# A step of self attention with its matrix products in another order

## The reference

```
scores = einsum('bhqd,bhkd->bhqk', q * 16**-0.5, k)      # 16 heads of 16 features
scores = where(causal, scores, finfo.min)
p   = softmax(scores, axis=-1)
ctx = einsum('bhqk,bhkd->bhqd', p, v)
```

## Time and profile before

| | us |
|---|---|
| median of three runs | 3683.33 |
| lowest and highest of them | 3674.78, 3687.11 |
| the profiled execution | 3663.53 |
| its span, from first to last instruction | 3661.7 |
| mean granted TensorE clock in the span | 0.972 of full |

### The profile page before, as it was taken

How to read it: one execution, slowest core, us unless ns; L and a number is a source line. 1 busy time by engine, 2 the same in 40 slices (tenths; PEclk the granted TensorE clock), 3 DMA queues, 4 the chain that set the end, 5 groups by cost and what they waited for, 6 DMA issues and landing times. The chain is left out here.

```text
span 3661.7 us, 74050 instructions
## 1 busy us (share of the span) xinstructions
PE 3383.0 (92%) x25048; PEld 2302.3 (63%) x25048; DVE 2019.3 (55%) x3324; ACT 1840.3 (50%) x3374; POOL 1590.0 (43%) x1421
## 2 busy tenths in 40 slices
PE   7777889898999799989999999999999998999997
PEld 5544644444444388866666666666666666878886
DVE  4454477777777455435555555555555553113454
ACT  2244357676776633435555555555555553333333
POOL 3211222121122111115777777777777776004554
PEclk9899989999999999999999999999999999999998
DMA  4765300000000123230010100000001002210200
GB/s 121 166 102 93 132 5 18 17 18 17 17 18 27 40 112 117 92 125 7 13 34 13 32 13 31 13 32 13 31 13 58 15 13 97 95 70 14 97 7 12
DMA packets 74751, 179.36 MB, mean 49 GB/s; under 512 B 14720, under 2 KB 44928, under 8 KB 68480
## 3 DMA queue, kind: packets, MB, share of 16 engines
q1 hardware_dynamic: 70240, 161.81, 14.6%
q0 software_dynamic: 4128, 12.60, 1.3%
HBM read 115.09 MB, written 59.26 MB: 48 GB/s over the span
## 5 line engine op out<-in xcount | busy, mean ns | idle before, releaser
L1688 POOL TENSOR_TENSOR cross_acc<-cross_acc,cross_probs 128x512 f32<-128x512 f32 (+1 forms) x704 | 921.4, 1309 | 160.1 <-ACT cross_probs L1751 118.6
L1751 ACT ACTIVATE cross_probs<-cross_s,cross_bias 128x512 f32<-128x512 f32 (+1 forms) x832 | 530.3, 685 | 489.4 <-PE cross_s L1970 485.8
L1847 DVE TENSOR_REDUCE cross_partmax<-cross_r 128x1 f32<-128x400 f32 (+1 forms) x1024 | 541.2, 570 | 334.7 <-PE cross_r L1940 316.3
L1290 DVE TENSOR_REDUCE cross_partmax<-cross_m 128x2 f32<-128x800 f32 (+1 forms) x512 | 497.1, 991 | 186.1 <-PE cross_m L1393 185.0
L1201 ACT ACTIVATE cross_probs<-cross_s 128x512 f32<-128x512 f32 (+1 forms) x832 | 453.9, 596 | 150.4 <-PE cross_s L1413 150.1
L1983 PE MATMUL cross_av<-cross_probs,cross_v 128*64 128x256 f32 (+1 forms) x3328 | 458.7, 393 | 0.0
L1983 PEld LDWEIGHTS cross_av<-cross_probs,cross_v 128*64 128x64 f32 (+1 forms) x3328 | 199.4, 136 | 172.7 <-ACT cross_probs L1751 77.0
L1140 POOL TENSOR_TENSOR cross_diag<-c_ident,cross_negmax 128x256 fp32r<-128x256 f32 x128 | 75.9, 615 | 495.5 <-DVE cross_negmax L1298 495.5
L1424 PE MATMUL cross_av<-cross_probs,cross_v 128*32 128x256 f32 (+1 forms) x3328 | 268.8, 395 | 10.4 <-ACT cross_probs L1201 8.9
L1964 PE MATMUL cross_s<-cross_q_hi,cross_k_hi 64*128 64x256 f32 (+1 forms) x1664 | 253.2, 299 | 0.0
L1836 DVE TENSOR_TENSOR cross_k_lo<-cross_r,cross_k_hi 128x400 fp32r<-128x400 f32 (+1 forms) x256 | 146.4, 572 | 191.6 <-ACT cross_k_hi L1729 191.6
(11 more groups left out here) (307 smaller groups left out, 6470.2 us busy)
## 6 DMA issues: line engine op xcount, KB each, us to landing
d_masked_ctx<-tail_ctx_split SPq DMA_DIRECT2D x8, 1602.0 KB, 5.3
d_self_qk<-selfproj_qk_split POOLq DMA_DIRECT2D x32, 256.0 KB, 5.5
self_qs<-d_self_qk SPq DMA_DIRECT2D x64, 128.0 KB, 8.5
self_ks<-d_self_qk SPq DMA_DIRECT2D x64, 128.0 KB, 9.1
d_cross<-tail_pr SPq DMA_DIRECT2D x8, 1024.0 KB, 4.6
cross_qp<-d_cross SPq DMA_DIRECT2D x64, 128.0 KB, 2.3
d_cross<-cross_out SPq DMA_DIRECT2D x64, 128.0 KB, 1.8
tail_attn<-d_cross SPq DMA_DIRECT2D x8, 1024.0 KB, 5.4
```

The lines of the kernel that those rows point to most:

```text
L1290: nc.vector.tensor_reduce(partmax[:, :, jt // 2, jt % 2, i:i + 1], m_pair(sets[q], w), AX.X, ALU.max).then_inc(maxed, 1)
L1688: nc.gpsimd.tensor_tensor(acc[0:w, g % 2], left, probs[0:w, slot % NPB], ALU.add).then_inc(added, 1)
L1751: nc.scalar.activation(probs[0:w, (g * KT + t) % NPB], src_, ACT.Exp, scale=XHD ** -0.5, bias=bias[0:w, p, t:t + 1]).then_inc(probs_ready, 1)
L1847: nc.vector.tensor_reduce(partmax[:, m, i:i + 1], r_ps[MAX_BANK[q]][:, 0:KCH[i][1]], AX.X, ALU.max).then_inc(maxed, 1)
```

## The change

Two calls move in TensorE's `step`. The other engines' code, all waits and all sizes stay as they are.

```
 def step(u, nxt):
     after = nxt and following(nxt, NG)
-    if after:
-        max_products(after, 0)
     if nxt:
         for t in range(2):
             score_products(nxt, t)
     if after:
+        max_products(after, 0)
         max_masks()
     if nxt:
         for t in range(2):
             score_shifts(nxt, t)
     if u[3]:
         sums(preceding(u, NG))
+    if after:
+        maxima(after, 1)
     values(u, 0)
     values(u, 1)
-    if after:
-        maxima(after, 1)
     if not nxt:
         sums(u)
```

## The result

| | before | changed |
|---|---|---|
| median of the first comparison (7 runs each), us | 3675.16 | 3647.49 |
| lowest and highest | 3667.09, 3687.11 | 3642.17, 3662.95 |
| span of the profiled execution | 3661.7 | 3645.7 |
| start of the last diagonals (line 575) | 349.56 | 328.71 |

The changed kernel is faster: ratio 0.9929, 95% interval 0.9907 to 0.9952. A second comparison on one chip gave 0.9940, 0.9918 to 0.9961. The prediction was 3656 us in 3645 to 3672; the measured median lies inside, and the gain of 27.7 us is that of the forecast, 27.5. What follows shows that two terms of the gain were wrong, in opposite directions, and that its agreement to 0.2 us is luck.

The account below looks back on a forecast made before the run. A loop through TensorE and VectorE, neither full, was taken to bound the phase. Shorter steps (23.5 us) plus fewer clock falls (4) gave 27.5, off the earlier runs' median 3683.33: 3656 us, range 3645 to 3672.

Parts of the forecast that it names:

- The loop: Step path through TensorE and VectorE: the values' 0.79 us leave it, so a step goes from 5.80 to 5.01 us.
- 1.73, 0.74, 0.06: Parts of a step, in us: shifts and sums; second maxima until the reductions; from the diagonals to the next shifts.
- VectorE's term, 2.48 us: Two reductions, the join of the maxima and the diagonals on VectorE, taken to stay at 2.48 us a step.
- the 23.5: Gain in the phase from shorter steps: 30 x 0.79 us less 0.2 us once in the first step.
- The clock: Five steps with a fall from 2.4 to 1.2 GHz cost 7.8 us; two or three were to go, gaining 4 us.
- The upper end: All five falls of TensorE's clock in the phase go: 7.8 us more, a gain of 31 us.
- The sum: Shorter steps and fewer clock falls in the phase together: 23.5 + 4 = 27.5 us gained.
- TensorE's cover: TensorE's spare time in each changed step, waiting for the diagonals before the shifts: 0.5 us.
- 0.32 for masks to values: Assumed time on TensorE from the start of the masks to the values, in us; bounds 0.2 and 0.6.
- Loads: Batches' queries and keys, loaded behind a store in about 19.4 us, were to stay hidden, barely.
- The margin of 3 us: Slack for batch 3's load before its first maxima: 22.4 us left for a load of 19.4 us.
- Score products: Moved in front of the first maxima, they wait for exponentials late only in the first step: 0.2 us, once.

Follow-up runs that it names:

- `maxima_first`: Kernel before with only the second maxima moved in front of the values, the score products left in place: 3653.01 us, ratio 0.9951.
- `pool_late`: Changed kernel with GpSimd's multiply held until VectorE has built the diagonals of the unit three later: 3642.17 us, ratio 0.9927 to the kernel before.
- `before_pool_later`: Kernel before, order kept, GpSimd's multiply held until three of four reductions of the unit three later are done: 3692.84 us in one execution.
- `scores_first`: Kernel before with only the next unit's score products moved in front of the first maxima: 3671.76 us, ratio 0.9999.
- `scores_twice`: Kernel before with score products moved in front of the first maxima and done twice there: 3669.44 us in one execution.

## Why the prediction was right, and where it was not

- **The loop.** Right in its parts: 1.73, 0.74, 0.06 are there to 0.01. The values left it: `maxima_first` shows it for the edit, and the steps of 5.01 in `pool_late` for the sum.
- **VectorE's term, 2.48 us.** Wrong; it measured 2.83. I had written that the change keeps the order in VectorE's and GpSimd's queues and took their durations with it. The order in each queue did stay, but not who is beside whom: before, the multiply ran beside the reductions; with the maxima 0.79 us earlier, line 572 comes while it runs. 29 x 0.34 = 9.9 us of the 23.5 were missed, and about 13.4 came. `pool_late` gives the 0.34 back in each step, `before_pool_later` adds 0.25 us to each step of the old order.
- **The clock.** Direction right, size too small: all five falls went, 7.8 us, where I took 4. The upper end, at which all five go, came true, but a shorter longest wait is not the reason: with it at 0.64 us the clock fell four times in `scores_first` and never in `scores_twice`. What differs there is TensorE's work, in one execution each.
- **The sum.** In the phase 13.4 + 7.8 = 21.2; measured 20.85, and the phase began 0.3 us later than before. The forecast was 27.5, too much by 6.6. The two comparisons gave 27.7 and 17.8, each with about 8 us either way, and 20.85 lies in both. That the first came so near 27.5 is luck.
- **TensorE's cover** was 0.81 us and not 0.5, because the step was 0.34 longer; in `pool_late`, with steps of 5.01, it was 0.47. The first maxima's products began at 3.79 behind the shifts (3.80 forecast) and their masks at 4.16. With 0.32 for masks to values I was right to 0.01 (236.13 - 235.81).
- **Loads.** Hidden, as forecast, with no wait in the phase. The margin of 3 us was too large. I had read 19.4 us for a load from windows of 2 us; by its landing time in the trace the load of batch 3 took 21.1 (200.14 to 221.20). In the changed kernel the five loads took 18.5 to 20.2 us and landed 2.8 to 4.9 us ahead of the first maxima; six intervals of 5.01 instead of 5.35 would have left 0.7 to 2.9. `pool_late`, whose multiply and so whose store come 1.8 us later (0.11 behind the next shifts, where it was 3.29 behind the last), used that up.
- **Score products.** They cost 0.3 us in the first step and earn nothing in this order; 0.2 was the forecast.

## What to carry to other kernels

Follow the loop through the engines and ask of each instruction in front of the hand-over whether the other engine needs it; one that isn't needed can go behind, and costs nothing there as long as the first engine still waits later in the step. When a term leaves a loop, the engines off the loop change places against it: look at which VectorE instructions with two inputs in SBUF now overlap with GpSimd instructions that read SBUF, since a tiny one can wait for a long one. Each step taken off exposes the next limit, here the loads' start, so move that with it.

## What the runs showed of the hardware

- VectorE's join of 4 elements a partition took 0.17 us alone and 0.50 beside a 0.73 us multiply of GpSimd, ending 0.03 us behind it; GpSimd's multiply took 1.79 us when it came 0.02 us behind a 1.23 us product on VectorE, and that product took 1.75 us when it came 0.07 us behind a multiply. Two reductions from PSUM took 1.02 us either way.
- TensorE's clock fell from 2.4 to 1.2 GHz five times in steps of 5.80 us with a longest wait of 1.1 us and four times with a longest wait of 0.64 us; with that same longest wait and the score products done twice in each step it did not fall. Each is one execution. A step with such a fall took 1.56 us longer.
- On TensorE a matmul of another kind (64 rows, 32 columns or the whole array) began 0.07 us before the modelled end of the one in front of it, in `before` and in the changed kernel; where the kind stays it was 0.16 (in the changed kernel's step, scores 236.92 + 0.68 to first maxima 237.44).
